# Edge one-hots of a graph kernel: stored by the first edge layer, loaded by the five later ones

## What is computed

```
# block 0 (one layer, "conv"): 2 heads, 128 wide, edge attributes of 32
alpha = sum(q[dst] * (k[src] + e)) / sqrt(C);  w = softmax of alpha over the edges of a dst
out   = segment_sum((v[src] + e) * w, dst)
# block 1 (three layers, "gat"): 4 heads of 64, 64 and 32
e     = leaky_relu(al_src[src] + al_dst[dst]);  out = segment_sum(softmax(e) * xp[src], dst)
# block 2 (one layer, "gatv2"): 4 heads of 32
e     = leaky_relu(sp[src] + dp[dst]);  attn = sum(double_attn * e);  out = segment_sum(sp[src] * alpha, dst)
# block 3 (one layer, "dot"): 4 heads of 32
e     = leaky_relu(sum(q[src] * k[dst]));  out = segment_sum(softmax(e) * v[src], dst)
```

## Time and profile before

| | us |
|---|---|
| median of three executions | 7668.35 |
| lowest, highest | 7663.28, 7670.11 |
| span of the profiled execution | 8869.1 |

### The profile page before, as it was taken

One profiled execution on the slowest core, in us unless ns is written; L12 is line 12 of the kernel. 1 busy time (PEld: TensorE's weight loads), 2 busy tenths in 40 slices (PEclk: granted clock), 3 DMA queues, 4 the chain that ended last, 5 costly groups with the idle time before them and its releaser, 6 DMA issues. The chain is left out here.

```text
span 8869.1 us, 129245 instructions
## 1 busy us (share of the span) xinstructions
PE 5045.4 (57%) x21094; PEld 3760.6 (42%) x21094; DVE 4591.5 (52%) x15579; ACT 5330.2 (60%) x14791; POOL 5197.0 (59%) x5195
## 2 busy tenths in 40 slices
PE   3888887445565635555634444554555554556555
PEld 2444444333343423433423444443544553455554
DVE  3666666434444634444533333364565555455555
ACT  1777777256666646666636666663666664566666
POOL 3556563266666466666556666635666663566664
PEclk7999999767666767666755555566777776677777
DMA  2222222134444334444322222201222222333342
GB/s 67 73 73 73 74 75 50 48 107 115 111 113 113 92 112 113 114 111 113 110 70 71 69 71 69 68 14 47 69 67 67 67 67 66 99 110 109 110 110 83
DMA packets 428332, 744.58 MB, mean 84 GB/s; under 512 B 207788, under 2 KB 248113, under 8 KB 427439
## 3 DMA queue, kind: packets, MB, share of 16 engines
q0 software_dynamic: 205312, 519.10, 23.0%
q1 hardware_dynamic: 218976, 215.57, 8.2%
q10 hardware_dynamic: 3280, 1.64, 0.1%
HBM read 718.36 MB, written 17.56 MB: 83 GB/s over the span
## 5 line engine op out<-in xcount | busy, mean ns | idle before, releaser
L476 POOL DMA_INDIRECT gat_ring<-tab,gat_ixb x2562 | 2579.9, 1007 | 1371.9 <-issue 769.0
L820 PE MATMUL gat_sc_ps<-gat_ring,gat_oh 128*128 128x264 f32 (+1 forms) x5124 | 1809.0, 505 | 600.4 <-issue 389.2
L820 PEld LDWEIGHTS gat_sc_ps<-gat_ring,gat_oh 128*128 128x128 f32 x5124 | 1184.6, 276 | 792.0 <-issue 656.8
L476 POOL DMA_INDIRECT conv_ring<-tab,conv_ixb x854 | 812.1, 951 | 655.3 <-issue 335.3
L476 POOL DMA_INDIRECT dot_ring<-tab,dot_ixb x854 | 833.1, 976 | 596.6 <-issue 272.1
L920 ACT ACTIVATE gat_oh<-gat_off,one 128x256 f32<-128x256 bf16 x1281 | 636.4, 497 | 857.2 <-PE gat_sc_ps L820 247.1
L476 POOL DMA_INDIRECT gatv_ring<-tab,gatv_ixb x854 | 831.5, 974 | 511.2 <-issue 237.9
L618 DVE TENSOR_TENSOR acc<-acc,gat_sc_ps 128x264 f32 (+1 forms) x1281 | 489.8, 382 | 1140.0 <-PE gat_sc_ps L820 318.2
L900 ACT ACTIVATE gat_off<-iota,rel 128x128 bf16<-128x128 f32 x2562 | 868.0, 386 | 0.1
L914 ACT ACTIVATE gat_ohT<-gat_offT,one 128x256 bf16<-128x256 bf16 x1281 | 633.9, 495 | 384.7 <-issue 271.2
L609 DVE TENSOR_TENSOR gat_ring<-gat_ring,gat_p_sb 128x520 f32<-128x520 f32 (+1 forms) x1281 | 769.6, 601 | 4.1
(11 more groups left out here) (455 smaller groups left out, 9991.0 us busy)
## 6 DMA issues: line engine op xcount, KB each, us to landing
gat_rel_row<-d_rel SPq DMA_DIRECT2D x216, 384.0 KB
gat_ring<-tab,gat_ixb POOLq DMA_INDIRECT x2562
conv_rel_row<-d_rel SPq DMA_DIRECT2D x72, 384.0 KB
gatv_rel_row<-d_rel SPq DMA_DIRECT2D x72, 384.0 KB
dot_rel_row<-d_rel SPq DMA_DIRECT2D x72, 384.0 KB
conv_ring<-tab,conv_ixb POOLq DMA_INDIRECT x854
conv_ring<-in_attr SPq DMA_DIRECT2D x427, 32.0 KB
gatv_ring<-tab,gatv_ixb POOLq DMA_INDIRECT x854
```

Source lines behind the costliest of these rows:

```text
L476: gp.indirect_dma_start(out=ring[:, r, t, 0:width], out_offset=None, in_=table[:, :], in_offset=bass.IndirectOffsetOnAxis(ap=ixb[:, r, t:t ...
L820: last = pe.matmul(sc_ps[:, m % SCB, 0:F], oh[:, m % 4, u, :], rows, start=(u == 0), stop=(u == 1))
```

## The change

The conv layer stores every group's one-hots in DRAM: the turned one in fp32 (128 KB) and in bf16 (64 KB), the plain one in fp32 (128 KB). The three DRAM tensors hold them in batches of four groups, 128 rows of four groups each. SP issues the three stores of a group, each after a wait for the one-hot, and ACT and DVE wait for the landing before they write a buffer again (three buffers of each kind, `OHB`). The bf16 copy is new work: DVE makes it from `offT` with one comparison (`turned_half`).

The five later layers make none. SP loads a batch of four turned one-hots (`turned_in`, bf16 in gat, fp32 in gatv2 and dot) and a batch of four plain ones (`plain_in`), two batches of each in SBUF; PE waits for a batch at its first group. ACT's `one_hots` is gone; conv has `turned_one_hot`, which holds both steps. The batches of target numbers in conv shrink from six groups to four.

SP's order in conv is new too: two batches of numbers and the attributes of the first three chunks are asked for ahead of the first store; then, group by group, the turned stores, the plain store of the group two chunks back, and the attributes of the next chunk's group, which wait for a scatter as before.

```diff
-RG = 6
+RG = 4
 RB = 2
+OHB = 3
...
-    rel_row = ph.sb("rel_row", [P, RB, RG, 2 * P], BF16)
-    OHB = 2 if conv else 4
-    ohT = ph.sb("ohT", [P, OHB, 2, P], BF16 if gat else F32)
-    oh = ph.sb("oh", [P, 4, 2, P])
-    offT = ph.sb("offT", [P, 2, 2 * P], BF16)
+    if conv:
+        rel_row = ph.sb("rel_row", [P, RB, RG, 2 * P], BF16)
+        ohT = ph.sb("ohT", [P, OHB, 2, P])
+        ohT16 = ph.sb("ohT16", [P, OHB, 2 * P], BF16)
+        oh = ph.sb("oh", [P, OHB, 2, P])
+        offT = ph.sb("offT", [P, OHB, 2 * P], BF16)
+    else:
+        turned = ph.sb("turned", [P, RB, RG, 2, P], BF16 if gat else F32)
+        plain = ph.sb("plain", [P, RB, RG, 2, P])
...
+            def keep_turned(n):
+                b = n % OHB
+                sp.wait_ge(s("ohT"), n + 1)
+                sp.dma_start(one_group(T.d_turned32, n), ohT[:, b].rearrange("p u e -> p (u e)")
+                             ).then_inc(s(f"turned32_out{b}"), 16)
+                sp.wait_ge(s("ohT16"), n + 1)
+                sp.dma_start(one_group(T.d_turned16, n), ohT16[:, b]).then_inc(s(f"turned16_out{b}"), 16)
+
+            def keep_plain(m):
+                sp.wait_ge(s("oh"), m + 1)
+                sp.dma_start(one_group(T.d_plain, m), oh[:, m % OHB].rearrange("p u e -> p (u e)")
+                             ).then_inc(s(f"plain_out{m % OHB}"), 16)
+
+            def turned_in(k):
+
+                behind(sp, s("ex"), RG * (k - RB + 1))
+                n = min(RG, NGR - RG * k)
+                sp.dma_start(turned[:, k % RB, 0:n].rearrange("p g u e -> p (g u e)"),
+                             (T.d_turned16 if gat else T.d_turned32)[k, :, 0:n * GE]).then_inc(s(f"turned_in{k % RB}"), 16)
+
+            def plain_in(k):
+
+                behind(sp, s("scat"), RG * (k - RB + 1))
+                n = min(RG, NGR - RG * k)
+                sp.dma_start(plain[:, k % RB, 0:n].rearrange("p g u e -> p (g u e)"), T.d_plain[k, :, 0:n * GE]
+                             ).then_inc(s(f"plain_in{k % RB}"), 16)
...
+            if conv:
+                for k in range(RB):
+                    numbers(k)
+                for ch in range(RING):
+                    for g in range(SIZES[ch]):
+                        attributes(ch, ch, g)
+            for i in range(NCH + 2):
+                for g in range(GC):
+                    n = BASE[i] + g if i < NCH and g < SIZES[i] else None
+                    m = BASE[i - 2] + g if i > 1 and g < SIZES[i - 2] else None
                     if conv:
-                        attributes(ch, ch % RING, g)
-                if gat and ch:
-                    landed(ch - 1)
-                if ch == RING and own_to is not None:
-                    for i in range(NG):
-                        own_rows(i, own_to)
-            if gat:
-                landed(NCH - 1)
+                        if n is not None:
+                            keep_turned(n)
+                            if n % RG == RG - 1 and RG * (n // RG + RB) < NGR:
+                                numbers(n // RG + RB)
+                        if m is not None:
+                            keep_plain(m)
+                            if i + 1 < NCH and g < SIZES[i + 1]:
+                                attributes(i + 1, (i + 1) % RING, g)
+                    else:
+                        if n is not None and n % RG == 0:
+                            turned_in(n // RG)
+                        if m is not None and m % RG == 0:
+                            plain_in(m // RG)
+                    if gat and g == 0 and 0 < i <= NCH:
+                        landed(i - 1)
...
             def one_hot(i, g):
                 m = BASE[i] + g
+                behind(v, s("scat"), m - OHB + 1)
+                if m >= OHB:
+                    v.wait_ge(s(f"plain_out{m % OHB}"), 16 * (m // OHB))
                 for u in range(2):
-                    last = v.tensor_scalar(oh[:, m % 4, u, :], T.iota[:], T.rel[:, bass.ds(m * 2 + u, 1)], None,
+                    last = v.tensor_scalar(oh[:, m % OHB, u, :], T.iota[:], T.rel[:, bass.ds(m * 2 + u, 1)], None,
                                            ALU.is_equal)
                 last.then_inc(s("oh"), 1)
+
+            def turned_half(i, g):
+
+                n = BASE[i] + g
+                if n >= OHB:
+                    v.wait_ge(s(f"turned16_out{n % OHB}"), 16 * (n // OHB))
+                v.wait_ge(s("offT"), n + 1)
+                v.tensor_scalar(ohT16[:, n % OHB, :], offT[:, n % OHB, :], 0.0, None, ALU.is_equal).then_inc(s("ohT16"), 1)
...
+                if conv:
+                    pe.wait_ge(s("ohT"), n + 1)
+                    which = ohT[:, n % OHB]
+                else:
+                    if n % RG == 0:
+                        pe.wait_ge(s(f"turned_in{n // RG % RB}"), 16 * (n // RG // RB) + 16)
+                    which = turned[:, n // RG % RB, n % RG]
...
+                if conv:
+                    pe.wait_ge(s("oh"), m + 1)
+                    which = oh[:, m % OHB]
+                else:
+                    if m % RG == 0:
+                        pe.wait_ge(s(f"plain_in{m // RG % RB}"), 16 * (m // RG // RB) + 16)
+                    which = plain[:, m // RG % RB, m % RG]
...
+                behind(a, s("ohT16"), n - OHB + 1)
                 a.nop(nofuse=True)
-                a.activation(offT[:, n % 2, :], rel_row[:, n // RG % RB, n % RG, :], ACT.Abs, bias=T.pid[:],
+                a.activation(offT[:, n % OHB, :], rel_row[:, n // RG % RB, n % RG, :], ACT.Abs, bias=T.pid[:],
                              scale=-1.0).then_inc(s("offT"), 1)
-
-            def one_hot(m):
-                for u in range(2):
-                    last = a.activation(off[:, m % 2, u, :], T.iota[:], ACT.Abs, bias=T.rel[:, bass.ds(m * 2 + u, 1)],
-                                        scale=-1.0)
-                last.then_inc(s("off"), 1)
-
-            def one_hots(i, g, reads, sums_):
-                n, m = BASE[i] + g if reads else None, BASE[i - 2] + g if sums_ else None
-                if reads:
-                    turned_one_hot(i, g)
-                if sums_ and not conv:
-                    one_hot(m)
-                if reads:
-                    a.wait_ge(s("offT"), n + 1)
-                    behind(a, s("ex"), (2 if conv else 1) * (n - OHB + 1))
-                    a.nop(nofuse=True)
-                    a.activation(ohT[:, n % OHB].rearrange("p u e -> p (u e)"), offT[:, n % 2, :], ACT.Relu, bias=T.one[:],
-                                 scale=-1.0).then_inc(s("ohT"), 1)
-                if sums_ and not conv:
-                    a.wait_ge(s("off"), m + 1)
-                    behind(a, s("scat"), m - 3)
-                    a.nop(nofuse=True)
-                    a.activation(oh[:, m % 4], off[:, m % 2], ACT.Relu, bias=T.one[:], scale=-1.0).then_inc(s("oh"), 1)
+                a.wait_ge(s("offT"), n + 1)
+                behind(a, s("ex"), 2 * (n - OHB + 1))
+                if n >= OHB:
+                    a.wait_ge(s(f"turned32_out{n % OHB}"), 16 * (n // OHB))
+                a.nop(nofuse=True)
+                a.activation(ohT[:, n % OHB].rearrange("p u e -> p (u e)"), offT[:, n % OHB, :], ACT.Relu, bias=T.one[:],
+                             scale=-1.0).then_inc(s("ohT"), 1)
...
-                    one_hots(i, g, g < read, g < summed)
+                    if conv and g < read:
+                        turned_one_hot(i, g)
...
+    T.d_turned16 = c.dram("d_turned16", [-(-NGR // RG), P, RG * GE], BF16)
+    T.d_turned32 = c.dram("d_turned32", [-(-NGR // RG), P, RG * GE])
+    T.d_plain = c.dram("d_plain", [-(-NGR // RG), P, RG * GE])
```

More of the change, by code:

```diff
@@ L517, in _ @@
-            if gat:
-                landed(NCH - 1)
+            if conv:
[8 more added lines that the diff above has]
+                    m = BASE[i - 2] + g if i > 1 and g < SIZES[i - 2] else None
+                    if conv:
+                        if n is not None:
[13 more added lines that the diff above has]
+                        landed(i - 1)
+                if i == RING and own_to is not None:
+                    for j in range(NG):
+                        own_rows(j, own_to)
@@ L794, in expand @@
                         at = t % 12 * 24
-                        last = pe.matmul(ex_ps[:, t // 12, at:at + 24], ohT[:, n % OHB, u, :], mine, start=True, stop=True)
+                        last = pe.matmul(ex_ps[:, t // 12, at:at + 24], which[:, u, :], mine, start=True, stop=True)
                     last.then_inc(s("ex"), 1)
@@ L808, in expand @@
                         pe.nop(nofuse=True)
-                        pe.matmul(ex_ps[:, 2 * (n % 2) + u, 0:F], ohT[:, n % OHB, u, :], mine, start=True, stop=True
+                        pe.matmul(ex_ps[:, 2 * (n % 2) + u, 0:F], which[:, u, :], mine, start=True, stop=True
                                   ).then_inc(s("ex"), 1)
@@ L819, in scatter @@
                     rows = msgs[:, m % 2, u, :] if conv else ring[:, r, 2 * g + u, W - F:W]
```

(2 more changed lines are left out.)

25 lines of the change are left out of this document (14 added, 11 removed).

## The result

The changed kernel takes 7767.11 us (7762.43 to 7773.96), the kernel before 7666.1 beside it (now four executions): 1.013 times as long, with a 95% interval of 1.0116 to 1.0145. It is 101 us slower, where 42 were forecast; 7767 lies inside the forecast's own case (7685 to 7790) and the range.

A forecast was written before the change was run, and what follows sets the result against it. The prediction took POOL's gathers to pace all six edge stages. Its terms, tails -15, loads 0, SP in conv +43, head +10 and end +4, summed to +42 on 7668, giving 7710 us, with a range of 7540 to 7850.

The forecast's parts named there:

- the forecast's own case (7685 to 7790): Whole kernel: the summed terms hold, 42 us slower at 7710 us; chance 0.46.
- Gathers pace the stages: All six edge stages: POOL's gathers set the pace in timed runs, 1.25 us each; ACT, PE and DVE keep up.
- The missing 1201 us: Profile of before: 13.5% of the 8869.1 us span taken as engine stops absent when nothing is recorded.
- the sum of 7642 us: Whole kernel before: gathers' busy and issue 6671, tails 240, the rest 731 us; 26 us from the median.
- ACT's one-hots at nothing while gathers run: Five later stages: taking 2.26 us a group off ACT is worth nothing while gathers pace them.
- the rival in which one-hots pace the later stages: Later stages: ACT's one-hots set the pace, so removing them gives 7430 to 7650 us; chance 0.18.
- Tails, -15: Five later stages after the last gather: 3 us a stage saved without ACT's one-hots, bounds 0 and -50.
- Loads at 0: Later stages: loading one-hots stays hidden and does not hold POOL up, 0 us; other end 20 us a stage.
- The bf16 half: Conv, DVE: new comparison of 0.2 us a group, 85 us on an engine with room; at most 85 us lost if gathers wait.
- SP in conv, +43: Conv, SP's queue: 2.4 of 2.69 us a group, hiccups partly absorbed, 0.1 us a group lost; bounds 0 and +150.
- the prediction's own rival: Conv: SP paces from 2.69 us a group; at 0.7 us a store it needs 3.3, giving 7790 to 7970 us; chance 0.11.
- Head, +10: Start of conv: 36 attribute loads ahead of the first store delay the fourth group's one-hot; bounds 0 to 37 us.

The follow-up runs named there:

- Third gather: Kernel before with one more indirect DMA a group in the third gat stage: 9544 us against 8965, ratio 1.0641.
- plain ones alone: Kernel before with conv storing only plain one-hots, in pairs with six buffers, later stages loading them, turned ones left to ACT: 7736 us against 7671, ratio 1.0093.
- fixed rows: Changed kernel with conv's attributes loaded from fixed rows, without SP's load of the row number: 8776 us against the kernel before's 8879, ratio 0.9879.
- the other two kernels timed on such chips: Pairs with later attributes, 7716 us against the kernel before's 7672, and plain ones alone, 7736 against 7671.
- pairs with later attributes: Changed kernel, conv's stores issued for two groups at once, four buffers, attribute loads between stores: 0.9906 and 0.9932 of the kernel before with pauses, 1.0058 without.

## Why the prediction was right and wrong

The sign, the place and the mechanism held: later stages paced by gathers, the loss in conv, SP's queue as what loses it. The size, 42 us of 101, was under half, and the step that failed is the price of SP's queue in conv: 2.4 us a group (the terms given, 1.12 + 1.1 + 0.1, make 2.32), where the trace has 2.74 to 2.81.

**Gathers pace the stages: right.** Third gather, plain ones alone, and POOL's waits of the changed kernel say the same, with one reserve: where everything pauses, freeing ACT still won 101 to 106 us. In conv of the changed kernel SP's queue sets the pace; for conv of the kernel before no profile without pauses tells.

**The missing 1201 us are stops made by the recorder: wrong,** and it cost the reading of the whole page its footing. The recorder doesn't make them: the changed kernel's recorded execution took 7771 us among others of 7762 to 7774, and on chips with pauses the other executions are as long as the profiled one. The stops themselves were read rightly, and the sum of 7642 us, which left them out, stands; that it fitted was no proof of where they come from. I also wrote that profiled later stages might fall and the times would not follow. On chips that pause the times do follow, by 101 and 106 us.

**ACT's one-hots at nothing while gathers run: right without pauses as far as shown** (1172 us with 47 us of ACT's work, 1171 with 431; all 826 were never profiled there), wrong with them. Plain ones alone speaks against the rival in which one-hots pace the later stages on the one kind of chip, the third gather on the other, and why 101 to 106 us were won there stays open. **Tails, -15: too much.** On one chip they went from 185 to 178 us. The tails of the changed kernel's own profile are shorter than those of the earlier trace rows because that chip doesn't pause, which is no gain of the change.

**Loads at 0: right.** Dot moves 203 GB/s at a share of 0.66, forecast 200 at 0.73, and gathers take 966 ns.

**The bf16 half: right in size and in effect.** The trace has it at 232 ns on average (forecast 200). Where the Trainium skill ("SBUF — State Buffer", "Who interferes with whom") would have such an operation lock out the writing of descriptors if it runs in a two-port mode, no lock shows here: conv's gathers take 951 ns with it, as before. Whether it ran in such a mode no run tells.

**SP in conv, +43: the term that was mis-sized.** Conv as a whole, head and end with it, grew by about 100, where 43 + 10 + 4 = 57 were forecast. I priced a store by the row of line 490, 344 ns. But those issues all stand behind a wait (of 4.8 to 8.6 us in the middle of the stage), and the record of a DMA that has waited is the shorter one. SP's store of the plain one-hots, with both kinds in it:

```profile
L517 SPq DMA_DIRECT2D d_plain<-conv_oh x427: 319/449/1996, 194.3 to 1425.6; - x143
```

Of its rows from 250 to 1300 us the 351 that follow the row ahead within 0.04 us have a median of 450 ns, the four that waited 320 each. Three stores are 1.5 us instead of 1.1, the attributes 1.2 instead of 1.12, and the sum of a group 2.74 to 2.81 instead of 2.4: past the 2.69 from which, by the prediction's own rival, SP decides. That rival had the mechanism and the point, and priced a store at 0.7, too dear. Taking 0.7 us of it away again (fixed rows) took all of the loss away, on a chip with pauses. How much of the 101 us is the queue's length, and how much the coupling by buffers, was not told apart. Nor was conv of the kernel before profiled on a chip without pauses. If the later stages gained nothing there, it took 1322 - 101 = 1221 us; the other two kernels timed on such chips give 1266 - 44 = 1222 and 1283 - 66 = 1217. That they agree shows that the three differ from each other in conv alone, and tests nothing about the kernel before. With the later stages as they are, conv grew by 0.24 us a group. An upper bound can be estimated: 854 gathers at 1.25 us and a tail of 53 make 1120 us, below which conv before can't have been, so the later stages can have gained 100 us at most, and conv lost 200.

**Head, +10: within its bounds.** The first store went out at 150.12, 41 us into the stage; moving the attributes gave some 23 us, roughly measured, on chips with pauses. **End, +4:** not measured by itself.

## What to carry to other kernels

A queue that issues DMAs in order is an engine: add up its instructions, the register loads between them too, at the price of an issue that did not wait (0.43 to 0.47 us here, and 0.8 for the row number), and compare that with the pace of the stage. Then look at what stands ahead of each store, because a store frees a buffer, and any wait ahead of it in the queue becomes a wait of the engine that writes the buffer. And set a profile's span against times of the same chip before you explain the difference.

## What the runs showed of the hardware that was not expected

Two conditions: the kernel before takes 7666 to 7672 us on some chips and 8879 to 9032 on others, and the changed kernel is 1.3% slower on the first and equal on the second (1.0004, 0.9994 to 1.0014). On the second kind the gathers themselves are as short as on the first (951 ns in conv) while the engines stop now and then, POOL for 2.8 us on average, SP for about 1 us in the lines shown and PE for 2.81 in the earlier trace rows. Whether this belongs to the chip or to the time at which it runs isn't known: no chip was seen in both conditions. A change that only takes work off an idle engine was worth 1.1 to 1.2% there; on the others it was not timed by itself. No version tried beats the kernel before on both: pairs with later attributes wins 0.7 to 0.9% on chips that pause and loses 0.6% where there are none.
